# Attention with shared keys: stacks loaded by DMA from spilled copies, score products in pairs

## What is computed

```python
def _L2_xattn_ref(q, k, v):           # layer 3 is the same
    NUM_Q_HEADS = 32
    NUM_KV_HEADS = 8
    D = E // H                        # 16 channels in a head
    scores = jnp.einsum('bkgsd,bktd->bkgst', qh, kh) / scale
    weights = jax.nn.softmax(scores, axis=-1)
    out = jnp.einsum('bkgst,bktd->bkgsd', weights, vh)
...
x = x + _L1_xattn_ref(_layernorm(x, axis=-1), ctx_512, ...)   # 16 heads of 32, causal
x = x + _L2_xattn_ref(_layernorm(x, axis=-1), ctx_512, ctx_512)
x = x + _L3_xattn_ref(_layernorm(x, axis=-1), ctx_512, ctx_512)
```

## Time and profile before

| | us |
|---|---|
| median of 3 runs | 4070.13 |
| lowest and highest | 4068.88, 4073.53 |
| the profiled execution | 4041.53 |
| its span (first to last instruction) | 4039.8 |

### The profile page before, as it was taken

One profiled execution on the slowest core, in us unless ns is written; L12 is line 12 of the kernel. 1 busy time (PEld: TensorE's weight loads), 2 busy tenths in 40 slices (PEclk: granted clock), 3 DMA queues, 4 the chain that ended last, 5 costly groups with the idle time before them and its releaser, 6 DMA issues. The chain is left out here.

```text
span 4039.8 us, 64864 instructions
## 1 busy us (share of the span) xinstructions
PE 3451.4 (85%) x18066; PEld 2386.6 (59%) x18070; DVE 2419.2 (60%) x4267; ACT 2054.4 (51%) x3563; POOL 898.4 (22%) x1818
## 2 busy tenths in 40 slices
PE   4349996899972799839999799899897999989998
PEld 2137775666651688714444367788775444436886
DVE  6964445455543333368888554666466788865665
ACT  5643333355531455427877633566433677774433
POOL 2410001544322100053333130122113333310000
PEclk8669998999986899959999899999998899999999
DMA  3424442400011333320000252577442000002223
GB/s 138 148 99 140 137 136 76 167 0 0 1 52 44 122 107 99 104 83 1 0 0 0 71 177 93 180 240 240 169 140 81 1 0 0 0 9 73 93 93 114
DMA packets 133100, 346.47 MB, mean 86 GB/s; under 512 B 15300, under 2 KB 15428, under 8 KB 132338
## 3 DMA queue, kind: packets, MB, share of 16 engines
q1 hardware_dynamic: 99666, 228.74, 17.5%
q0 software_dynamic: 22480, 96.23, 7.0%
q10 hardware_dynamic: 10864, 20.45, 1.4%
HBM read 274.58 MB, written 68.16 MB: 85 GB/s over the span
## 5 line engine op out<-in xcount | busy, mean ns | idle before, releaser
L1338 DVE TENSOR_REDUCE at_maxima<-psum 128x1 f32<-128x512 f32 (+1 forms) x1280 | 813.5, 661 | 288.8 <-PE psum L1148 134.8
L1309 ACT ACTIVATE at_probs<-psum 128x512 f32<-128x512 f32 (+3 forms) x1280 | 692.8, 570 | 352.1 <-PE psum L1159 200.4
L1144 PE MATMUL psum<-at_kT,at_qT 64*128 64x512 f32 (+2 forms) x1280 | 555.7, 480 | 14.9 <-DVE at_kT L1351 8.8
L1159 PE MATMUL psum<-at_qT_max,at_kT 64*128 64x512 f32 (+4 forms) x1280 | 533.0, 454 | 27.9 <-ACT at_probs L1309 23.3
L1159 PEld LDWEIGHTS psum<-at_qT_max,at_kT 64*128 64x128 f32 (+1 forms) x1280 | 218.3, 186 | 341.8 <-ACT at_probs L1309 294.6
L573 PE MATMUL psum<-f_xT_hi,ffn_w_hi 128*128 x1024 | 405.2, 396 | 9.0 <-DVE f_xT_lo L2050 2.2
L573 PE MATMUL psum<-f_xT_lo,ffn_w_hi 128*128 x1024 | 404.4, 395 | 0.0
L1176 PE MATMUL psum<-at_probs,at_vals 128*32 128x512 f32 (+4 forms) x2560 | 375.7, 578 | 2.1 <-issue 2.1
L1112 PE MATMUL psum<-ident,at_arr 128*128 128x128 f32 x1536 | 255.8, 292 | 97.2 <-POOL at_arr L1015 94.9
L1112 PEld LDWEIGHTS psum<-ident,at_arr 128*128 128x128 f32 x1536 | 169.2, 145 | 200.9 <-POOL at_arr L1015 96.2
L1003 POOL TENSOR_TENSOR at_gap<-ones 128x1 f32<-128x1 f32 x448 | 87.2, 195 | 850.3 <-DVE at_result L1365 600.0
(11 more groups left out here) (379 smaller groups left out, 7264.7 us busy)
## 6 DMA issues: line engine op xcount, KB each, us to landing
ffn_w_raw<-in_stream SPq DMA_DIRECT2D x262, 256.0 KB, 2.8
ffn_w_hi<-quantized SPq DMA_DIRECT2D x66, 512.0 KB, 3.5
ffn_w_hi<-quantized SPq DMA_DIRECT2D x65, 256.0 KB, 3.1
ffn2a_w_raw<-in_shared2a SPq DMA_DIRECT2D x26, 512.0 KB, 3.6
ffn2b_w_raw<-in_shared2b SPq DMA_DIRECT2D x26, 512.0 KB, 3.6
qz_raw<-in_stream SPq DMA_DIRECT2D x17, 768.0 KB, 4.3
quantized<-qz_quant POOLq DMA_DIRECT2D x16, 768.0 KB, 3.5
gathered<-zeros SPq DMA_DIRECT2D x1, 12288.0 KB
```

The costliest lines, as they stand in the source:

```text
L1144: mm = pe.matmul(bank[:, 0:width], qT[ring % 2][rows_of(h), h // HPS, t * P:(t + 1) * P], kT[ring][rows_of(h), h % 2, 0:width], start=True ...
L1159: mm = pe.matmul(bank[:, 0:S - lo], kT[ring][rows_of(h), h % 2, t * P:(t + 1) * P], qT_max[ring % 2][rows_of(h), h // HPS, lo:S], start=Tr ...
L1309: act.activation(probs[n % RING][:, 0:S - lo], scoreT[n % 2][:, 0:S - lo], ACT.Exp, scale=factor).then_inc(exped, 1)
L1338: dve.tensor_reduce(maxima[:, t, h:h + 1], (score + scoreT)[n % (4 if first else 2)][:, 0:width], AX.X, ALU.max).then_inc(maxed, 1)
```

## The change

at2 and at3 are computed by a new function, `stage_attend_shared`. The norm before them now makes `xT` as the other layers do (with PSUM banks 4 to 7, argument `bank`). SP writes both parts of it to DRAM, `q_hi` and `q_lo`, two transfers of 1 MB for each batch; `stage_keys_values` writes the parts of the context, `k_hi` and `k_lo`, in layer 1. From there SP loads the stacks already turned: 12 transfers for a group, each of 16 rows of 2 KB or twice that. The maxima are not put into a stack of tokens but into a small tile (`split`), of which four transposes make two rows a head; ACT moves them to `maxT` and SP puts them into rows 48 and 49 of the q stacks by four transfers (`put_max`). S is issued as two products behind every second T, into a pair of PSUM banks, and one reduction of DVE takes the maxima of both. q, k and the values need no copies on POOL other than 64 columns of values.

In at1 the widths of S become 128, 256, 384 and 512, and all mask products have 128 columns.

```diff
@@ stage_attend, at1 @@
-                width = min(S, P * (t + 2 - t % 2)) if causal else S
+                width = P * (t + 1) if causal else S
...
-                    m = 2 * P if t % 2 == 0 else P
-                    mm = pe.matmul(bank[:, t * P:t * P + m], ident16[:, :], mask[:, 0:m], start=False, stop=True, skip_group_check=True)
+                    mm = pe.matmul(bank[:, t * P:(t + 1) * P], ident16[:, :], mask[:, :], start=False, stop=True, skip_group_check=True)
@@ new: stage_attend_shared @@
+    HD, H, PARTS = HEAD2, 4, 3
+    USED = PARTS * HD
+    HALF = P // 2
+    PAIRS = H * TB
+    SETS = PAIRS // 2
+    RING, SLOTS = 2 * H, 4
+    LOADS, PUTS = 2 * PARTS * 2, H
+    LAST, VALUES, MAX, RES = 1, (5, 9, 13), 5, 9
...
+        score, scoreT, res, turn = [room.psum[:, 1024 * m:1024 * m + 1024] for m in range(2)], room.banks[4:6], room.banks[6], room.tiles(7)
...
+        def head_tile(n):
+            return n // (PAIRS // 2), 1 - n % 2, n % (PAIRS // 2) // 2
...
+        def spill(sp, b):
+            sp.wait_ge(made, before + TB * (b + 1))
+            part = slice(b * S, (b + 1) * S)
+            for dst, src in zip((q_hi, q_lo), xT):
+                sp.dma_start(dst.rearrange("(c p) t -> p c t", p=P)[:, :, part], src[:, :, part].bitcast(F32)).then_inc(spilled, DMA)
...
+            def load(place, j):
+                b, n = batch_piece(place, j)
+                r, tokens = place % SLOTS, bass.ds(b * S, S)
+                for par in range(2):
+                    for i, src in enumerate((q_hi, q_lo, q_hi)):
+                        at = HALF * par + HD * i
+                        rows = src[n * H * HD:(n + 1) * H * HD, tokens].rearrange("(jj par d) t -> par d jj t", jj=2, par=2)
+                        sp.dma_start(qT[r][at:at + HD, :, :].bitcast(F32), rows[par]).then_inc(landed[r], DMA)
+                    for i, src in enumerate((k_hi, k_hi, k_lo)):
+                        at = HALF * par + HD * i
+                        sp.dma_start(kT[r][at:at + HD, :].bitcast(F32), src[n * HD:(n + 1) * HD, tokens]).then_inc(landed[r], DMA)
+            def put_max(place, j, g):
+                r = place % SLOTS
+                sp.wait_ge(max_moved, g + 1)
+                for jj in range(2):
+                    for par in range(2):
+                        at = HALF * par + USED
+                        row0 = 2 * (2 * jj + 1 - par)
+                        sp.dma_start(qT[r][at:at + 2, jj, :].bitcast(F32), maxT[place % 2][row0:row0 + 2, :]).then_inc(put[r], DMA)
+            spill(sp, 0)
+            sp.wait_ge(spilled, 2 * DMA)
+            for g in range(SLOTS - 1):
+                load(g, 0)
+            for b in range(1, B):
+                spill(sp, b)
+            put_max(0, 0, 0)
+            sp.wait_ge(spilled, 2 * B * DMA)
+            def slot(s, place, j, ahead):
+                if ahead >= 3:
+                    if not is_first(s):
+                        sp.wait_ge(scoredT, PAIRS * s)
+                    load(place + 3, j)
+                if ahead >= 1:
+                    put_max(place + 1, j, s + 1)
...
+            def scores(g, place, j, n):
+                jj, par, t = head_tile(n)
+                r, m = place % SLOTS, n // 2
+                if n == 0:
+                    pe.wait_ge(landed[r], LOADS * DMA * (use(place, j) + 1))
+                if n % 2 == 0:
+                    pe.wait_ge(maxed, SETS * g + m + 1)
+                mm = pe.matmul(score[m % 2][:, 512 * (n % 2):512 * (n % 2) + S], qT[r][half(par, USED), jj, t * P:(t + 1) * P],
+                               kT[r][half(par, USED), :], start=True, stop=True)
+                if n % 2 == 1:
+                    mm.then_inc(scored, 1)
+            def scores_T(g, place, j, n):
+                t, h, r = n // H, n % H, place % SLOTS
+                if n == 0:
+                    pe.wait_ge(put[r], PUTS * DMA * (use(place, j) + 1))
+                pe.wait_ge(exped, PAIRS * g + n + 1)
...
+            for g in range(2):
+                for n in range(PAIRS):
+                    scores(g, g, 0, n)
+                    if g == 1 and n == MAX:
+                        pe.wait_ge(made, before + N // P)
+                        turn_max(0, 0)
+            def slot(s, place, j, ahead):
+                first = is_first(s)
+                for n in range(PAIRS):
+                    scores_T(s, place, j, n)
+                    if ahead >= 2 and n % 2 == 1:
+                        scores(s + 2, place + 2, j, n - 1)
+                        scores(s + 2, place + 2, j, n)
+                    if n == LAST and not first:
+                        results(s - 1, place + 3, TB - 1)
+                    if n in VALUES:
+                        results(s, place, VALUES.index(n))
+                    if n == MAX and ahead >= 1:
...
+                        turn_max(s + 1, place + 1)
+                    if n == RES and not first:
...
+                        turn_results()
... ACT: move_res behind the exp of n = 2, move_max behind that of n = 6
... DVE: max_set reduces 128 x 2 x 512; split_maxima; finish behind set 5
```

More of the change, by code:

```diff
@@ L226, in repeat, with stage_norm @@
         sp.wait_ge(self.repeated, DMA)
-def stage_norm(k, nm, xT=None, tokens=None, rows=None, joined=None, beside=None, before=None):
+def stage_norm(k, nm, xT=None, tokens=None, rows=None, joined=None, beside=None, before=None, bank=0):
     with stage_room(k, joined) as room:
@@ L1521, in _, with stage_keys_values @@
             take(B - 1, TB - 1)
-def stage_keys_values(k, nm, ctxT, weights, k_g, v_g, joined=None):
+def stage_keys_values(k, nm, ctxT, weights, k_g, v_g, k_hi, k_lo, joined=None):
     PIECES = k_g.shape[1] // B
@@ L1549, in _, with batch @@
             sp.dma_start(c_raw[:, N:N + S], ctxT[:, 0:S]).then_inc(c_landed, DMA)
+            for s in range(2):
+                sp.sem_inc(kept[s], 2 * DMA)
+            def batch(b, s):
+                sp.wait_ge(c_lo_made, b + 1)
+                for dst, src in ((k_hi, c_hi), (k_lo, c_lo)):
+                    sp.dma_start(dst[:, bass.ds(b * S, S)], src[s][:, :].bitcast(F32)).then_inc(kept[s], DMA)
+            in_turn(sp, batch)
+            for s in range(2):
+                sp.wait_ge(kept[s], (B + 2) * DMA)
         @block.tensor
@@ L1583, in batch @@
                     act.activation(place(k_g, b, t), out[0][t % 2][:, :].rearrange("p (n f) -> p n f", n=PIECES), ACT.Copy).then_inc(k_taken, 1)
-            split(0, 0)
-            in_turn(act, batch)
+            split(0, 0, 0)
+            with act.Fori(0, B // 2) as j:
+                for s in range(2):
+                    batch(2 * j + s, s, j)
         @block.vector
@@ L2429, in _, with gather_beside, queries @@
                     combiner.gather(pool, range(2))
-                def gather_beside(pool, b, made, before):
+                def gather_beside(pool, b):
                     if b + 2 < B:
                         combiner.gather(pool, range(b + 2, b + 3))
-                    beside(pool, b, made, before)
-                return stage_norm(k, "n4", tokens=lambda b, t: of_batch(q_g, b, t), joined=room, beside=gather_beside, before=combiner.add_batch)
+                return stage_norm(k, "n4", xT=xT, joined=room, beside=gather_beside, before=combiner.add_batch, bank=TB)
             for layer in (2, 3):
-                with ExitStack() as q_ctx:
[L2440 to L2450, removed]
+                def queries(room, xT):
+                    (low, _), _, _ = combine_and_norm(room, xT) if layer == 2 else stage_norm(k, "n6", xT=xT, joined=room, bank=TB)
+                    return low, TB
+                stage_attend_shared(k, f"at{layer}", ctx_g, scratch["q_hi"], scratch["q_lo"], scratch["k_hi"], scratch["k_lo"],
+                                    1.0 / np.sqrt(HEAD2), queries)
+                with ExitStack() as q_ctx:
+                    flat_q = k.sb(q_ctx, f"a{layer}_q", [P, NT * D]) if layer == 2 else None
                     if layer == 2:
+                        rows = flat_q[:, :].rearrange("p (t d) -> p t d", t=NT)
                         slots, homes = (k.sb(q_ctx, f"f2_{n}", [P, TOP2, NT], I32) for n in ("slots", "homes"))
```

225 lines of the change are left out of this document (200 added, 25 removed).

## The result

| | before | changed |
|---|---|---|
| median of 4 runs | 4069.51 us | 4373.06 us |
| lowest and highest | 4067.53, 4073.53 | 4343.49, 4406.24 |
| granted clock, whole span | 0.923 | 0.832 |

The ratio is 1.0746 with a 95% interval of 1.0691 to 1.0800. The forecast was 4123 us, range 4066 to 4175: the sign was right and the size wrong by a factor of nearly six, +304 us for +53.

A forecast was written before the change was run, and what follows sets the result against it. The prediction took a latency loop between T and exp to bound at2's slots, not PE throughput. Slots +54, starts +11 and 0, at1 -12 gave +53 us on the median of 4070.1: 4123 us, range 4066 to 4175.

The forecast's parts named there:

- The clock is no case of its own: Slots of at2 and at3: full clock assumed, since slots 29 and 30 had it with less PE work; no time added.
- The slot's sum: Slot of at2 and at3: 4 x 3.32 + 1.16 + 0.96 = 15.40 us against 14.55, +0.85; bounds 13.3 to 15.9.
- a plain leg: at2 and at3, from the T behind one R to that behind the next: 3.08 + 0.24 for paired S = 3.32 us.
- a term of 1.16: Two blocks of transposes right behind R each delay the next T by 0.58 us: 1.16 a slot, bounds 0 and 2 x 0.82.
- a term of 0.96: ACT's two moves, behind exp 2 and exp 6, each put off the following exp by 0.48 us: 0.96 a slot.
- The free block of the earlier trace: Last slot of at3: a leg without S takes 3.08 us although a block of transposes lies in it, so free there.
- the last part of the forecast: Signs in the profile after; the forecast is wrong if R and the transposes behind it take no more than R alone.
- Loads and put_max: SP's 16 issues a slot at 0.54 us plus 2.2 landing, 10.8 us, stay hidden; decides from 0.82 an issue.
- Rival 4: SP's chain becomes the slot in at2 and at3: at 0.9 us an issue 16.6 us, 4192 in all; chance 0.12.
- DVE: Eight reductions of 1226 ns, 9.8 us, plus some 1.1 stay below the slot of 15.4 us: costs nothing.
- The starts: Norm to first T: at3 +11 us (bounds 0 and 20), put_max waiting behind spills; at2 0 (bounds -3 and +12).
- at1: Narrower S and mask products save about 0.45 us a slot over 31 slots: -12 us, bounds -15 and -4.

## Why the prediction was wrong

**The step that failed** is this sentence: "The clock is no case of its own: it was granted in full in slots 29 and 30 too, where PE had less to do." Those two slots of one trace were taken for every slot of another kernel. The change took away rows, blocks and density at once. With 50 rows slot 30 of the kernel before runs at a mean clock of 0.57, and in the changed kernel even 64 rows did not always hold it there (0.63 and 0.70). In place of the full clock the runs show 0.68 in the slots of at2 and at3, which took 629.9 and 629.5 us, against 503.5 and 494.2 with 64 rows. No rival had the clock in it, so the range could not hold the time.

**What the clock costs.** At nearly full clock (0.98) at3's slots took 494 us (64 rows) and in the changed kernel 629.5. 135 us of its +166 are the clock's, 31 are the slot's. At2's took 503.5 (at 0.96) against 629.9. That is 126 + 135 = 261 of the 340 us by which the span grew, and somewhat less than the whole price, since the runs with 64 rows had dips of their own.

**What brings the clock down.** Rows in both products, rows in one, a repeated product, single S and transposes moved away from R each brought it back, in whole or in part. So neither the number of rows nor the order decides alone. What quantity stands behind them all stays open.

**The slot's sum was right, its split less so.** At full clock, in the run with 64 rows: a plain leg takes 3.33 us (2037.12 to the T at 2040.45; forecast 3.32), the leg with the results 4.37 (forecast 3.32 + 0.58 + 0.48 = 4.38), the one with the maxima 4.40. Two plain ones and these two make 15.43. But moving the blocks away from R gave 1.60 us for a term of 1.16, and moving ACT's two moves 0.39 for a term of 0.96; the two errors lie in opposite directions, and the sum does not show them. The free block of the earlier trace rows was indeed no rule for blocks behind R: from R to the next T it is 1.59 us with a block between and 0.99 without, as the last part of the forecast asked. These rows hold both (R, the transposes, T):

```profile
2041.60 1.07 PE L1554 MATMUL psum<-at_probs,at_vals 128*32 128x512 f32 x8
2042.59 0.50 PE L1541 MATMUL psum<-at_qT,at_kT 64*128 64x512 f32 x2
...
2045.41 1.07 PE L1554 MATMUL psum<-at_probs,at_vals 128*32 128x512 f32 x8
2046.41 0.66 PE L1561 MATMUL psum<-ident,at_split 128*128 128x128 f32 x4
2047.00 0.50 PE L1541 MATMUL psum<-at_qT,at_kT 64*128 64x512 f32 x2
```

**Loads and put_max.** Rival 4 is out. In the slot shown above SP issued the twelve loads from 2066.11 on, at 0.33 to 0.46 us each, and then put_max:

```profile
2076.30 2.41 SPq L1495 DMA_DIRECT2D at_qT<-at_maxT  x4
```

0.60 us an issue (forecast 0.54, deciding point 0.82), and in the steady slots no T waited for a transfer, not even at 12.49 us a slot. The rule of the Trainium skill on small transfers (page "DMA: Bandwidth & Descriptors", section "Bandwidth") did not decide the time here: sixteen a slot were hidden, and how fast they might have run was not measured. The 2 us for each, which the prediction took from the same page, are given there for transfers issued by GpSimd; SP's loads of 64 KB landed 2.2 to 2.3 us after their issue.

**DVE.** The new reduction takes 1223 ns (forecast 1226, from another operation of the same size); DVE's busy time is 10.66 us of the slot of 12.50 shown above (forecast 10.9):

```profile
L1649 DVE TENSOR_REDUCE at_maxima<-psum 128x2 f32<-128x1024 f32 x512 | 624.2, 1223 | 548.0 <-PE psum L1529 539.4
```

**The starts.** In at3 the first T came 58.0 us after the first clear, before it was 51.4 after the norm's start: +6.6 for a forecast of +11 (bounds 0 and 20). The reason was right, since it waited for put_max, which SP had issued right behind the last six spills:

```profile
3325.85 0.80 PE L1540 MATMUL psum<-at_qT,at_kT 50*128 50x512 f32 x2 [9.54 <-DMA at_qT<-at_maxT]
```

At2 began 6.7 us sooner behind at1, beyond my bound of -3. **at1**: -13.4 for -12. The step of 0.06 us for 128 columns holds, eight of them a slot; "in proportion" was more than the earlier trace rows gave, where 256 columns take 0.23 us and 128 take 0.16.

**Not of the change.** Most of the +18.0 us between at2 and the norm of at3 is a stall in the first feed-forward stage, where ACT waited 6.6 and 7.0 us; one of these waits stands ahead of a weight (`ffn2a_w_hi`), and that it came late is my reading. In eight other profiled runs that stretch was 13 to 27 us longer than before, among them the kernel before with 50 rows; four had none, nor had the profiled execution of the kernel before. The missing stall may be why it was 0.7% shorter than its median; this is argued, not shown.

## What to carry to other kernels

Before an edit takes work away from TensorE in a loop that waits on latencies, make the clock a rival with its own price: all of PE's steps of the slot at half the level, here 22.95 us for 15.43. Here less work in the array was slower than more, and unused rows or a repeated product in a wait was a cheap trial that showed it. Then shorten the loop: put nothing behind the step in which the other engine runs dry, and put that engine's side jobs inside it.

## What the runs showed that I had not expected

- In the changed kernel the granted clock depended on how many rows the products use, and not only on when PE is busy: with the same instructions at the same places it was 0.68 with 48 and 50 rows, 0.79 and 0.80 with T at 64, and 0.96 and 0.98 with both at 64, though the added rows of q hold only zeros.
- PE was busy for 89% of the changed kernel's slots by the profile (560 of 630 us) at a clock of 0.68, and for 82% (406 of 494 us) with 64 rows at 0.98: the busy share, which is longer because each product is slower, did not tell which of the two held its clock.
- Slots can settle in a length of their own: seven slots in a row took 16.8 to 17.0 us, each with one dip in it, where without the dip a slot is 15.43. That the dip and the length hold each other is argued, not shown.
